# Layer 0 of a four-layer kernel: a smaller state selector, biases loaded one section earlier, scatters issued without a pace

## The reference, cut to what matters

```python
xn = _layernorm(x, axis=-1)
x = x + _L0_attn_ref(xn, ...) + _L0_ffn_ref(xn, ...)

def _L0_attn_ref(inputs, ...):
    x_and_res = inputs @ W_in
    x, res = jnp.split(x_and_res, 2, axis=-1)
    x = silu(_depthwise_conv_same(x, K_conv, b_conv))
    delta, Bm, Cm = jnp.split(inputs @ W_x, [DT_RANK, DT_RANK + D_STATE], axis=-1)
    delta = softplus(delta @ W_dt + b_dt)
    y = _selective_scan(x, delta, A, Bm, Cm, D)   # h = exp(delta A) h + delta u B;  y = sum over states of C h
    return (y * silu(res)) @ W_out + b_out

def _L0_ffn_ref(x, ...):
    xn = _rmsnorm(x_flat, norm_weight, EPS)
    logits = xn @ router_weight.T + router_bias
    gate_vals, expert_idx = top_k(softmax(logits), 2)
    # each token goes to its slot in its two experts, comes back and is summed with its weights
```

## Time and profile before

| | us |
|---|---|
| median of three runs | 2064.2 (2059.05 to 2064.88) |
| the profiled execution | 2064.66, of which the span of its instructions 2062.9 |
| norm0, from the first statistic to the first instruction of front | 6.1 to 44.05 |
| front | 44.05 to 184.53 |
| scan, to the first instruction of the next section | 184.53 to 819.62 |
| layers 1 to 3 | from 819.62 |

### The profile page before, as it was taken

How to read it: one execution, slowest core, us unless ns; L and a number is a source line. 1 busy time by engine, 2 the same in 40 slices (tenths; PEclk the granted TensorE clock), 3 DMA queues, 4 the chain that set the end, 5 groups by cost and what they waited for, 6 DMA issues and landing times. The chain is left out here.

```text
span 2062.9 us, 35961 instructions
## 1 busy us (share of the span) xinstructions
PE 1561.3 (76%) x12142; PEld 1061.5 (51%) x12143; DVE 1368.0 (66%) x2390; ACT 1038.1 (50%) x1842; POOL 811.3 (39%) x779
## 2 busy tenths in 40 slices
PE   3983888888866666438688889994399999649994
PEld 3752666666644444416466666662134444347883
DVE  7635788787799998577333338877783499536334
ACT  1464877887754454134333336662264577524440
POOL 3277555565598884066211114342030000014005
PEclk9995999999998878578899999996689999859997
DMA  4311111111011010255311113420541132111322
GB/s 130 96 65 54 31 46 54 37 44 45 16 26 29 25 25 20 95 160 176 109 43 44 44 40 78 91 48 18 162 84 57 30 68 52 53 48 42 94 70 78
DMA packets 154088, 130.35 MB, mean 63 GB/s; under 512 B 19697, under 2 KB 138633, under 8 KB 153683
## 3 DMA queue, kind: packets, MB, share of 16 engines
q1 hardware_dynamic: 141394, 104.58, 18.3%
q0 software_dynamic: 12544, 23.82, 4.1%
HBM read 77.08 MB, written 52.43 MB: 63 GB/s over the span
## 5 line engine op out<-in xcount | busy, mean ns | idle before, releaser
L677 POOL TENSOR_TENSOR xn_t<-xn_t,scan_du 128x512 f32<-128x512 f32 x256 | 320.7, 1268 | 175.8 <-ACT xn_t L819 99.0
L722 PE MATMUL banks<-scan_hc,ident 128*128 128x256 f32 x1024 | 297.6, 417 | 72.0 <-DVE scan_hc L874 72.0
L868 DVE TENSOR_TENSOR_SCAN xn_t<-banks,xn_t 128x512 f32<-128x512 f32 x256 | 311.5, 1217 | 41.5 <-ACT banks L809 35.2
L2246 ACT ACTIVATE att_pr<-banks 128x768 f32<-128x768 f32 (+1 forms) x256 | 234.4, 917 | 129.1 <-PE banks L2139 77.3
L809 ACT ACTIVATE banks<-delta,scan_exp_centre,a_neg 128x255 f32<-128x255 f32 x512 | 265.3, 559 | 44.1 <-DVE xn_t L868 43.8
L722 PEld LDWEIGHTS banks<-scan_hc,ident 128*128 128x128 f32 x1024 | 194.5, 209 | 135.2 <-DVE scan_hc L874 100.3
L874 DVE TENSOR_TENSOR scan_hc<-xn_t,banks 128x512 f32<-128x512 f32 x256 | 175.9, 687 | 27.2 <-PE banks L707 16.5
L928 POOL DMA_INDIRECT disp<-xn_tok,places x128 | 133.9, 1046 | 106.1 <-PE banks L406 46.6
L2286 DVE TENSOR_REDUCE att_mb<-banks 128x4 f32<-128x1024 f32 x128 | 154.1, 1222 | 13.8 <-PE banks L2106 8.7
L2155 PE MATMUL banks<-att_pr,att_vx 128*32 128x256 f32 (+1 forms) x2048 | 155.3, 376 | 4.8 <-ACT att_ot L2251 3.3
L2106 PE MATMUL banks<-att_ks,att_qs 48*128 48x256 bf16 (+1 forms) x1024 | 111.7, 276 | 54.9 <-PEq L76 48.2
(11 more groups left out here) (341 smaller groups left out, 3356.6 us busy)
## 6 DMA issues: line engine op xcount, KB each, us to landing
att_ks<-k_parts SPq DMA_DIRECT2D x384, 32.0 KB
scan_ew<-f_packed SPq DMA_DIRECT2D x12, 578.0 KB
q_parts<-qk_parts SPq DMA_DIRECT2D x16, 384.0 KB, 2.6
k_parts<-qk_parts SPq DMA_DIRECT2D x16, 384.0 KB, 3.8
att_qs<-q_parts SPq DMA_DIRECT2D x64, 96.0 KB
gau_ew<-f_packed SPq DMA_DIRECT2D x8, 578.0 KB, 4.1
disp<-zeros SPq DMA_DIRECT2D x1, 4608.0 KB, 14.0
att_xin<-disp SPq DMA_DIRECT2D x72, 64.0 KB, 1.8
```

The source lines that it names most:

```text
L677: nc.gpsimd.tensor_tensor(bu[:, i % RING], b_sb[:, q % 2], du[:, b % 2, c:c + 1, :].to_broadcast([P, 2, T]), ALU.mult).then_inc(s.bu_made, 1)
L722: ins = nc.tensor.matmul(bank(Y_BANK)[:, c, :], g.ident[:], hc[:, i % RING, n, :], start=False, stop=(i % (PAIRS * DC) == PAIRS * DC - 1 a ...
L868: v.tensor_tensor_scan(rows(h[:, i % 2]), g.ps[:, DA + i % RING, :], rows(bu[:, i % RING]), 0.0, ALU.mult, ALU.add).then_inc(s.scan_done, 1)
L2246: nc.scalar.activation(pr[:, i % RING], g.ps[:, at:at + 2, 0:W], ACT.Exp, scale=scale).then_inc(s.p_ready, 1)
```

## The change

It makes three edits in layer 0.

1. `sel` shrinks to 96 x 32. The memset and the three affine selects run over 32 values per partition in place of 4096, and the matmuls of L698 and L707 take one column, broadcast to 128 with a step of zero, as the stationary operand.
2. `b_conv` and the router's bias are loaded by `weights` in norm0, ahead of `w_in` and the taps, on a semaphore of their own, `bias_in`. In front ScalarE (before its first Silu) and DVE (before the routing) wait for both. The section front loses these two DMAs.
3. `pace` is gone: GpSimd waits for `r_placed` and then issues all 64 scatters back to back.

```diff
-    AT_COUNT, AT_SIGMOID, AT_SCATTER = 3, 3, 7
+    AT_COUNT, AT_SIGMOID = 3, 3
@@ front, sync
-                sp.dma_start(bc[:], t["m_b_conv"]).then_inc(s.w_in, 16)
-                job.sync(sp)
@@ front, gpsimd
                 pool.wait_ge(s.r_placed, 1)
-
-                def pace(i):
-                    if i < 12:
-                        pool.wait_ge(s.xz_ready, AT_SCATTER + i // 2)
-                scatter(nc, pool, scattered, g.xn, disp, r, 2, pace=pace)
+                scatter(nc, pool, scattered, g.xn, disp, r, 2)
@@ front, scalar
-                act.wait_ge(s.w_in, 16)
+                act.wait_ge(r.bias_in, 32)
@@ state_selection
-        v = sel[2 * DS * q:2 * DS * (q + 1), :, :]
+        v = sel[2 * DS * q:2 * DS * (q + 1), :]
         nc.gpsimd.affine_select(out=v, in_=v, compare_op=ALU.not_equal, fill=1.0, base=0,
-                                pattern=[[-1, 2 * DS], [0, P]], channel_multiplier=1).then_inc(filled, 1)
+                                pattern=[[-1, 2 * DS]], channel_multiplier=1).then_inc(filled, 1)
@@ scan
+        def row(i):
+            return sel[:, i:i + 1].to_broadcast([3 * 2 * DS, P])
-                        ins = nc.tensor.matmul(bank(BO)[:, n, :], sel[:, 2 * pr + n, :], bc3[:, b * T:(b + 1) * T],
+                        ins = nc.tensor.matmul(bank(BO)[:, n, :], row(2 * pr + n), bc3[:, b * T:(b + 1) * T],
-                        ins = nc.tensor.matmul(bank(C_BANK)[:, n, :], sel[:, DS + 2 * pr + n, :],
+                        ins = nc.tensor.matmul(bank(C_BANK)[:, n, :], row(DS + 2 * pr + n),
@@ routing, vector
-        if biased:
+        if title == "route0":
+            dve.wait_ge(r.bias_in, 32)
+        elif biased:
             dve.wait_ge(s.r_in, 16)
@@ layer0
-        sel = l.enter_context(nc.sbuf_tensor("state_sel", [3 * 2 * DS, 2 * DS, P], BF16))
+        sel = l.enter_context(nc.sbuf_tensor("state_sel", [3 * 2 * DS, 2 * DS], BF16))
             def weights(sp):
+                sp.dma_start(r.bias[:], t["f0_router_b"].to_broadcast([P, E0])).then_inc(m.bias_in, 16)
+                sp.dma_start(f.bc[:], t["m_b_conv"]).then_inc(m.bias_in, 16)
                 sp.dma_start(f.w[:], t["m_w_in"]).then_inc(m.taps_in, 16)
```

More of the change, by code:

```diff
@@ L294, in mamba_front @@
     NEAR = (E0 - FIRST_MLP0) * CAP0
-    with section(nc, "front", *ROUTE, "w_in", "xz_ready", "gate_ready", "gate_out0", "gate_out1", "act_done", "biased",
+    with section(nc, "front", *ROUTE, "xz_ready", "gate_ready", "gate_out0", "gate_out1", "act_done", "biased",
                  "b_out_in", "near_in", "delta_in", "dt_ready", "dtx_done", "z_ready", "zb_done", "high_done", "rem_done",
                  "copied", "split_done", "abs_done", "exp_done", "ln_done", "delta_done", "neg_a") as s:
-        bc = s.sb("b_conv", [P, DC])
         gate = s.sb("gate", [P, 2, DC, T])
@@ L453, in _ @@
                         ins = nc.scalar.activation(u[:, c, b * T:(b + 1) * T], g.ps[:, 2 * p, c * T:(c + 1) * T],
-                                                   ACT.Silu, bias=bc[:, c:c + 1])
+                                                   ACT.Silu, bias=f.bc[:, c:c + 1])
                     ins.then_inc(s.act_done, 1)
@@ L942, in routing @@
     biased = title in ("route0", "route1")
-    bias = sb("bias", [P, E])
+    bias = r.bias if title == "route0" else sb("bias", [P, E])
     rev = sb("rev", [P, E])
@@ L978, in sync @@
     def sync(sp):
-        if title == "route0":
-            sp.dma_start(bias[:], t["f0_router_b"].to_broadcast([P, E])).then_inc(s.r_in, 16)
         if title == "route1":
@@ L2663, in layer0 @@
         gate_d = nc.dram_tensor("gate0", (P, DC, N), F32, kind="Internal").ap()
-        m = l.enter_context(section(nc, "moe0", "sel_set", "scattered", "taps_in", "taps_scaled", "scan_in"))
+        m = l.enter_context(section(nc, "moe0", "sel_set", "scattered", "taps_in", "taps_scaled", "scan_in", "bias_in"))
         u = l.enter_context(nc.sbuf_tensor("u", [P, DC, N], F32))
@@ L2674, in layer0 @@
         r.row = t["f0_norm"].to_broadcast([P, D])
+        r.bias = l.enter_context(nc.sbuf_tensor("router_bias0", [P, E0], F32))
+        r.bias_in = m.bias_in
         f = Names()
@@ L2680, in layer0 @@
         with ExitStack() as c:
+            f.bc = c.enter_context(nc.sbuf_tensor("b_conv", [P, DC], F32))
             f.w = c.enter_context(nc.sbuf_tensor("w_in_sb", [P, 2 * DI], F32))
```

## The result

The kernel after takes 2040.76 us (median of 4 runs, 2037.87 to 2046.0), the kernel before beside it 2064.54 (4 runs); the ratio is 0.9893 [0.9866, 0.992]. The profiled execution of after took 2037.87, its span is 2036.2, against 2062.9 before: 26.7 us less.

A forecast was written before the change was run, and what follows sets the result against it. In layer 0, DVE, held by GpSimd's affine selects, bounds norm0 and GpSimd's paced scatters bound front; −6.05 − 17.7 + 0 + 0 = −23.7 takes the profiled 2064.66 to 2041.0, median 2040.5 us, range 2034.5 to 2048.

The forecast's parts named there:

- norm0, −6.05: norm0: small selector frees DVE of 7.95 us of stalls, less 1.9 lost; net −6.05, within −7.95 and −5.55.
- the three steps: norm0: DVE's L171, L174, L176, held by GpSimd for 3.01, 3.29, 2.20 us, would lose 7.95 in all.
- collision: norm0: the taps' product on GpSimd (L2691) would meet DVE's L171; loss 0 to 2.4 us, 1.9 taken.
- Biases, 0: Front: DVE's routing starts some 3 us earlier but waits longer for the count matmuls; 0 us.
- The scatters: Front: without pace, first issue 25.4 us after front's start, one of about 4.3 beside L508, last over at 156.8.
- other holds: Front: 2.60 us of the old scatter queue, beyond plain issues, pace and L527, assumed to stay.
- DVE last, slack of 2.5 us: End of front: DVE still ends at 165.82, scan starts at 166.85; GpSimd's 164.3 is 2.5 us ahead.
- The broadcast columns, 0: Scan: the 512 bf16 loads of L698 and L707 with a step of zero cost nothing; 0 us.
- The drain does not grow: End of front: GpSimd's queue drain, 5.28 us, stays when scatters come closer; growth would prove the prediction wrong.
- The sum: Whole kernel: −6.05 − 17.7 + 0 + 0 = −23.7 us, all in layer 0.
- my rivals: Scatters last in front 0.14; broadcast loads slow in part 0.06, slower than before 0.04; scan's waits leave no gain 0.02.
- −17.7: Front: taking out the pace starts scan at 166.85 and not 184.53, −17.7 us.

The follow-up runs named there:

- two pauses: Kernel after with two waits put among GpSimd's scatters, the first of which never came: 2042.58 us, ratio 0.9875.
- second group: Four follow-up runs on one chip like that of the forecast; the kernel before took 2067.79 us there (19 runs).
- short rows: Kernel after, each scatter writing 128 bytes a row in place of 512, as many scatters and rows: 2042.26 us.
- before again: The kernel before, unchanged, profiled again on a chip like that of the forecast: 2069.1 us, ratio 1.0005 to itself.
- edit 3 alone: Kernel before with only the scatters' pace taken out: 2146.7 us, ratio 1.0082.
- the three kernels with pauses: Kernel after with two pauses, 2042.58 us; with the pauses moved, 2047.76; with moved pauses, added TensorE matmuls and the taps' product in pieces, 2041.71.
- first group: Four follow-up runs on one chip, unlike that of the forecast; the kernel before took 2127.86 us there (13 runs).
- the selector alone: Kernel before with only the small selector, old bias loads and old pace kept: 2120.14 us, ratio 0.9961.

## Why the prediction was right, and where it was not

The forecast was 2040.5 us, the median is 2040.76. By its own steps:

- **norm0, −6.05, measured −2.84: mis-sized by what it left out.** The mechanism was right in each piece: stalls of the three steps gone but for a collision of 2.17 us (1.9 forecast). I took DVE as the last engine of norm0 after the edit as before it. I did not ask what TensorE's level would be when it starts at 19.75 and not at 25.55, and that its matmuls at the lower level would end 2.9 us behind DVE. Profiles at like levels give back the forecast term: upper level, 44.04 before to 37.73 (two pauses) is −6.31; lower level, 46.89 (before, second group) to 40.88 (short rows) is −6.01. Either kernel can be at either level: TensorE of before ran its router matmuls at 0.96 in the first profile and at 1.73 in the second group's.
- **Biases, 0: right.** L1001 has no wait for a DMA, and L1043 waits 3.81 us for the counts where its like waited 2.09.
- **The scatters: right, with smaller holds.** First issue 24.5 us after the start of front (25.4 forecast), one issue of 4.04 us (4.3). From first to last they took 85.2 us where 87.4 were forecast: I kept 2.60 us of other holds, and 0.75 were left, since four issues took 1.40 before, the first of them beside L504, and now none but the first and the 4.04 takes over 1.08. The 4.04 beside L501 and the 1.40 beside the old L504 both speak against what the Trainium skill, "SBUF — State Buffer", section "Who interferes with whom", infers, that a `tensor_tensor` leaves descriptors alone. Whether the issue is held at the write of its descriptors or at a read in SBUF, no run here shows.
- **DVE last, slack of 2.5 us: right in kind.** The slack is 163.24 − 150.89 − 7.50 = 4.85. Front shrank by 18.45; the 0.75 beyond the forecast fit the first batch of TensorE, whose taps take 5.47 and not 6.32 us; the granted clock rises 3.7 us after front's start here (44.9) and rose 5.4 after it before (49.4).
- **The broadcast columns, 0: right.** 103 and 102 ns. Scan took 636.8 to 641.3 us with them, and 635.1, 642.7 and 641.1 without them (before, before again, edit 3 alone): no cost is to be seen beside that spread.
- **The drain does not grow:** 5281 ns with scatters close together, on either kind of chip (5286 in the three kernels with pauses).
- **The sum was right in part by luck.** Layer 0 gave 19.55 us in this pair and not 23.7; layers 1 to 3, whose code is the same, were 7.2 us shorter in the same pair. In a pair of the second group, before again and short rows, the end of scan moved from 829.38 to 801.18 (28 us). The change is worth 20 to 28 us of layer 0 in these pairs, and 23.7 is in the middle of what two single profiles can show.
- **What the prediction had no place for** is the first group's chip. There edit 3 is not −17.7 but +18.8 us alone against before, and +21.4 as after against the selector alone (2141.55 − 2120.14), and the whole change +0.6%. None of my rivals was this mechanism: I took a wait on GpSimd for a pure cost because no row showed what else it did. In the earlier trace rows nothing could have shown it, since on the forecast's chip TensorE's signals are on time with the pace and without it.

What is shown: on the chip of the first group the semaphores that TensorE raises go up as much as 67 us late while scatters run freely, ScalarE and DVE wait for them, and TensorE then waits for these two; the signals are on time again once the scatters are over, and with the pace front is 17 to 20 us shorter. It is neither a want of instructions nor the transfer of `gate`. What is open: what holds the signals and TensorE's instructions back (the recording of the profile itself is not excluded), why on that chip, and whether a pause or two among the scatters would be enough; the kernels made for that question ran on chips where it doesn't come up.

## What to carry to other kernels

Before a wait that only "paces" an engine is taken out, ask what else lives in the gaps that it makes, and measure on more than one chip: here the same kernel was 24 and 26 us faster than before in two groups of runs and 14 us slower on another chip. When engines stand still, read first which semaphore ended the wait and when the work that raises it was over, and set anything that comes "late" beside its place in the program. Price an edit by the section it is in, but then ask again which engine is last at the new start, and at which clock level. A small matrix with a broadcast column got rid of 15 us of fills here at no cost to be seen in scan. A queue that is not last can be moved by its slack (4.85 us here) at no cost, and not by more.

## What the runs showed of the hardware

- GpSimd's queue, having issued 64 indirect DMAs, drains for 5281 to 5286 ns at the end of front, whatever the spacing of the scatters.
- A scatter of 32 packets is issued in 0.97 us every 1.28, with 512 bytes a row or with 128. One begun beside a `tensor_tensor` of DVE that takes 4.42 us takes 4.04.
- On one chip, beside scatters every 1.28 us, the semaphores of finished matmuls went up as much as 67 us late (their readers start 0.03 to 0.1 us behind them in before and after on the chip of the forecast), and TensorE came to start one matmul every 2.80 us, where it starts one every 0.22 us otherwise.
- TensorE's clock level in norm0 differs from run to run of the same kernel (router groups at 0.96 or 1.73 us), it was at the upper one where 18.3 us of zero matmuls came before them, and 3.0 us won there were all but gone at the end of scan.
